# A two-layer decoder on one core: expert stages over tokens sorted by expert instead of all experts over all tokens, and gated scores computed per head

## Reference, cut to what matters

```
x = LN(x + self_attention(LN(x)))          # 16 heads of 64                      stage A
x = LN(x + cross_attention(x, ctx))        # 16 heads, 77 context rows           stage B
x = LN(x + experts(x))                     # 8 experts, width 512, gelu, the best 2 of 8      stage C
x = LN(x + gated_linear_attention(x))      # 16 heads, decay per head and row    stage D
x = LN(x + cross_attention(x, ctx))        # 8 heads                             stage E
x = LN(x + experts(x))                     # 8 experts, width 256, relu, the best 1 of 8      stage F
```

## Time and profile before

| | us |
|---|---|
| median of 3 runs | 1707.96 (1705.93 to 1708.29) |
| the profiled execution | 1707.19 |
| its span, first to last instruction | 1705.4 |
| TensorE busy | 1535.0, 90% of the span |
| VectorE, ScalarE, GpSimd busy | 964.6, 916.6, 455.8 |
| mean granted TensorE clock | 0.973 of full |

### The profile page before, as it was taken

The page is one execution under the profiler, slowest core; times in us unless marked ns, Lnnn a source line. Parts: engine busy times, 40 slices in busy tenths (PEclk is TensorE's granted clock), DMA queues, the critical chain, the costliest instruction groups (busy, mean ns, idle before and its releaser), DMA issues.

```text
span 1705.4 us, 21767 instructions
## 1 busy us (share of the span) xinstructions
PE 1535.0 (90%) x6814; PEld 833.2 (49%) x6864; DVE 964.6 (57%) x2740; ACT 916.6 (54%) x1889; POOL 455.8 (27%) x385
## 2 busy tenths in 40 slices
PE   6999999999999888878999988998889897786997
PEld 2334443444443354544555555666565663453554
DVE  3443544543443446576665647667666766466675
ACT  4777677677677354553444445556454543353433
POOL 2555455455455123230000002222222221121000
PEclk9999999999999989999999999999999997897999
DMA  4000000000000200001000000000000000100000
GB/s 145 1 1 1 1 1 1 1 1 1 1 1 1 75 25 1 0 1 62 1 0 1 1 25 1 1 1 1 1 1 1 1 1 1 50 1 0 1 13 13
DMA packets 13504, 18.56 MB, mean 11 GB/s; under 512 B 832, under 2 KB 9808, under 8 KB 13264
## 3 DMA queue, kind: packets, MB, share of 16 engines
q1 hardware_dynamic: 12816, 16.06, 3.0%
q10 hardware_dynamic: 576, 1.11, 0.2%
HBM read 16.11 MB, written 1.05 MB: 10 GB/s over the span
## 4 chain that ended last, share of the span: by engine, by line
PE 71%; DVE 16%; ACT 6%; issue 5%; POOL 0%; DMA 0%; POOLq 0%; DVEq 0%; ACTq 0%
PE bank L624 8%; PE bank L443 7%; PE bank L425 7%; PE bank L376 6%; PE bank L433 6%; PE bank L759 3%; PE bank L415 3%; PE bank L505 3%; PE bank L519 2%; PE bank L725 2%; PE bank L607 2%; PE bank L755 2%; PE bank L609 2%; PE bank L608 2%; PE bank L548 2%
## 5 line engine op out<-in xcount | busy, mean ns | idle before, releaser
L1719 POOL TENSOR_TENSOR work<-work 128x512 f32<-128x512 f32 x256 | 266.2, 1040 | 269.3 <-DVE work L1279 269.3
L892 ACT ACTIVATE work<-bank,work 128x512 f32<-128x512 f32 x256 | 176.6, 690 | 117.1 <-DVE work L1271 117.0
L1053 ACT ACTIVATE work<-bank,cols 128x512 f32<-128x512 f32 x192 | 131.8, 687 | 189.7 <-PE bank L609 189.0
L1271 DVE TENSOR_REDUCE work<-bank 128x1 f32<-128x512 f32 x256 | 176.6, 690 | 76.0 <-PE bank L425 75.7
L624 PE MATMUL bank<-work,W 128*128 128x512 f32 x384 | 199.4, 602 | 3.9 <-DVE work L1503 3.8
L1503 DVE TENSOR_TENSOR work<-work,bank 128x512 f32<-128x512 f32 x192 | 130.0, 686 | 125.1 <-ACT work L1053 123.8
L433 PEld LDWEIGHTS bank<-cst,work 128*128 128x128 f32 x1024 | 110.5, 141 | 164.5 <-issue 103.7
L1279 DVE RECIPROCAL work<-work 128x1 f32<-128x1 f32 x256 | 41.8, 163 | 223.6 <-ACT work L892 223.3
L433 PE MATMUL bank<-cst,work 128*128 128x128 f32 x1024 | 159.9, 283 | 6.7 <-ACT work L900 6.1
L900 ACT ACTIVATE work<-bank 128x512 f32<-128x512 f32 x256 | 152.7, 597 | 0.5 <-PE bank L433 0.5
L425 PE MATMUL bank<-work 64*128 64x512 f32 x512 | 144.5, 641 | 3.4 <-ACT work L892 3.4
(11 more groups left out here) (215 smaller groups left out, 2687.1 us busy)
## 6 DMA issues: line engine op xcount, KB each, us to landing
W<-in_w1T SPq DMA_DIRECT2D x1, 2048.0 KB, 8.0
x_all<-in_x SPq DMA_DIRECT2D x4, 256.0 KB, 8.7
W<-in_L_attn_Wq SPq DMA_DIRECT2D x2, 512.0 KB, 4.3
W<-in_L_attn_Wv SPq DMA_DIRECT2D x2, 512.0 KB, 6.7
W<-in_L_attn_Wo SPq DMA_DIRECT2D x2, 512.0 KB, 8.8
W<-in_L_ffn_W SPq DMA_DIRECT2D x1, 1024.0 KB, 5.8
out<-x_all SPq DMA_DIRECT2D x4, 256.0 KB, 2.3
W<-in_L_attn_Wk ACTq DMA_DIRECT2D x1, 512.0 KB, 7.7
```

What stands on the lines that cost most here:

```text
L892: A(pA[u % 5], bank[u % 3][:, :], ACT.Exp, bias=nmax[:, u % 8:u % 8 + 1], accum_out=rsum[0][:, u % 8:u % 8 + 1]).then_inc(sem("a_e"), 1)
L1053: A(hsC[i % 3], bank[i % 3][:, :], m_["func"], bias=col(m_["b1"], s)).then_inc(sem(n + "_h"), 1)
L1271: V.tensor_reduce(nmax[:, u % 8:u % 8 + 1], bank[u % 3][:, :], AX, ALU.max, negate=True)\
L1719: G.tensor_tensor(pA[u % 5], pA[u % 5], rsum[1][:, u % 8:u % 8 + 1].to_broadcast([P, S]), ALU.mult)\
```

## The change

**Experts.** The router now runs for all four sequences first, and makes for each (token, choice) pair a rank within its expert: prefix sums by TensorE (`moe_prefix`), counts by VectorE (`moe_rank`). GpSimd scatters each row of x, 128 rows per indirect DMA, to a DRAM tensor `xs`, in which each expert has its own 2048 rows (`moe_scatter`: 32 DMAs in stage C, 16 in F). `moe_map` works out from the counts which expert each of at most 39 (stage C) or 23 (stage F) tiles of 128 rows belongs to. Then, per tile: GpSimd gathers 128 rows from `xs` (three buffers); SP reads the expert's number into a register and loads that expert's whole weights with both biases (128x1156 or 128x642 elements, seven buffers); TensorE transposes the rows, makes ft hidden slices of 128x128 and the output tile, all float32, one matmul each; ScalarE applies the activation with the bias; VectorE copies the transposed rows and adds b2; SP stores the tile to `ys` in DRAM. At the end GpSimd gathers each pair's row back (`moe_gather`: 32 DMAs in C, of which 16 within stage D, and 16 in F) and VectorE adds them, weighed, to x and normalises (`close_x`). The DRAM tensor `xs` is zeroed early, by ten DMAs on SP during stage A.

**Order.** Routing of sequences 0 and 1 moves into the cross stage before, the scatter of sequence 0 too; `close_x` of sequences 1 to 3 of stage C moves into stage D, at g = 0, 4, 8. Stage D now begins behind `close_x` of sequence 0.

**Gated scores.** `qbD` and its GpSimd pass go. Each head's scores are four 128x128 matmuls over its own 64 rows, heads alternating, into a bank per head.

```diff
@@ SP @@
+            def moe_put(J):
+                sp.wait_ge(sem("M_y"), J + 1)
+                j = J % TILES0
+                sp.dma_start(T["ys"][j * P:(j + 1) * P, :], yM[J % 3]).then_inc(sem(f"M_ys{J % 3}"), 16)
...
+                for j in range(m_["tiles"]):
+                    J = m_["j0"] + j
+                    e = sp.value_load(em[0:1, j:j + 1], min_val=0, max_val=E - 1)
+                    if j >= NW:
+                        moe_put(J - NW)
+                    sp.dma_start(wM[J % NW][:, 0:m_["wide"]], T[m_["w"]][:, bass.ds(e, 1), :])\
+                        .then_inc(sem(f"M_w{J % NW}"), 16)
@@ TensorE @@
-                mm(out[:, :], high, xh_M[b % 2], start=True, stop=False)
-                mm(out[:, :], low, xh_M[b % 2], start=False, stop=False)
-                mm(out[:, :], high, xl_M[b % 2], start=False, stop=True).then_inc(sem(n + "_hp"), 1)
+                for f in range(m_["ft"]):
+                    m = mm(out[:, f * P:(f + 1) * P], wM[J % NW][:, f * P:(f + 1) * P], xTM[J % 2], start=True, stop=True)
...
+                for f in range(ft):
+                    m = mm(out[:, 0:D], hTM[J % 3][:, f * P:(f + 1) * P], wM[J % NW][:, (ft + f) * P:(ft + f + 1) * P],
+                           start=(f == 0), stop=(f == ft - 1))
...
+                for j in range(n + 3):
+                    if j < n:
+                        moe_turn(m_, j)
+                    if 1 <= j <= n:
+                        moe_h(m_, j - 1)
+                    if j >= 3:
+                        moe_y(m_, j - 3)
...
-                        m = mm(out[:, (c % 2) * 256:(c % 2 + 1) * 256], kTD[g % 2][:, c * P:(c + 1) * P],
-                               qbD[g % 2][:, c * 256:(c + 1) * 256], start=True, stop=True)
-                    m.then_inc(sem("d_s"), 1)
+                    for hh in range(2):
+                        m = mm(out[hh][:, r], kTD[g % 2][HALF[hh], r], qTD[g % 2][HALF[hh], r], start=True, stop=True)
+                m.then_inc(sem("d_s"), 1)
@@ VectorE @@
+                dve.wait_ge(sem(f"M_g{b}"), 16 * NT * 2 + 16 * NT * (m_["b0"] // NB))
+                for k in range(m_["k"]):
+                    for t in range(NT):
+                        i = V.scalar_tensor_tensor(out=res[:, t, :], in0=gathered(m_, b, t, k), scalar=w[:, t, k:k + 1],
+                                                   in1=(res if k else x)[:, t, :], op0=ALU.mult, op1=ALU.add)
...
+                ln_stats(res)
+                ln_apply(res, x).then_inc(x_ready, 1)
@@ GpSimd @@
+                        G.indirect_dma_start(T["xs"], bass.IndirectOffsetOnAxis(s1[:, pair(m_, b, t, k)], 0),
+                                             x_all[:, 4 * b + t, :], None).then_inc(sem("M_sc"), 16)
...
+                pool.wait_ge(sem("M_sc"), 16 * NB * NT * (2 + m_["b0"] // NB))
+                for j in range(m_["tiles"]):
+                    J = m_["j0"] + j
+                    if J >= 3:
+                        pool.wait_ge(sem("M_xtp"), J - 2)
+                    G.indirect_dma_start(xgM[J % 3], None, T["xs"], bass.IndirectOffsetOnAxis(xi[:, j:j + 1], 0))\
+                        .then_inc(sem(f"M_x{J % 3}"), 16)
...
+                for b in range(2 if ph == 2 else NB):
+                    moe_gather(m_, b)
...
-                    G.tensor_tensor(qbD[g % 2].rearrange("p (c h i) -> p c h i", c=NT, h=2), q, own, ALU.mult)\
-                        .then_inc(sem("d_qb"), 1)
-
+                    if g in (1, 5):
+                        moe_gather(MOE[2], 2 + g // 5)
```

More of the change, by code:

```diff
@@ L200, in decoder @@
         wqB, wkB, wvB, woB = (W1[:, i * 1024:(i + 1) * 1024] for i in range(4))
-        w1C, w2C = W0[:, 0:4096], W0[:, 4096:8192]
+        wM = [W0[:, i * WIDE:(i + 1) * WIDE] for i in range(NW)]
         woD = W1[:, 4096:5120]
@@ new lines, in moe @@
+                tail(m_["w0"] - 1, 0)
+                moe_prefix(m_, 2)
+                for s in range(1, 5):
+                    tail(m_["w0"] - 1, s)
+                moe_logits(m_, 3)
+                moe_prefix(m_, 3)
+                n = m_["tiles"]
+                for j in range(n + 3):
[5 more added lines that the diff above has]
+                        moe_y(m_, j - 3)
@@ L825, in _ @@
             moe(5)
-            for s in range(32):
-                tail(WORKS - 1, s)
         @block_ctx.scalar
@@ new lines, in moe @@
+                n, ft = m_["tiles"], m_["ft"]
+                moe_rank(m_, 1)
+                moe_route1(m_, 2)
+                moe_route2(m_, 2)
+                for s in range(3):
+                    tail(m_["w0"] - 1, s)
+                moe_rank(m_, 2)
+                for s in range(3, 5):
+                    tail(m_["w0"] - 1, s)
+                moe_route1(m_, 3)
+                moe_route2(m_, 3)
+                moe_rank(m_, 3)
+                enter(dve, ph)
+                moe_map(m_)
```

606 lines of the change are left out of this document (339 added, 267 removed).

## The result

The changed kernel takes **1638.89 us** (median of 4 runs, 1635.87 to 1640.13) against 1706.95 for the kernel before (4 runs on the same chip, 1705.93 to 1708.29): ratio 0.9598, 95% interval 0.9585 to 0.9612. The profiled execution has a span of 1638.3 us and a mean granted clock of 0.912 (0.973 before).

A forecast was written before the change was run, and what follows sets the result against it. TensorE, busy 90% of the span, was taken as the bound: 1705.4 - 61 (stage C) + 0 (D) - 21 (E, F) + 7 (clock) = 1630.4, plus 1.8 outside the span: 1632 us, range 1600 to 1660, chance 0.53.

The forecast's parts named there:

- p = 1.3: GpSimd's queue: each indirect DMA of 128 rows costs GpSimd 1.3 us, taken from its pass over 128 partitions.
- Rival 3: GpSimd's queue: indirect DMAs are dear, 3.3 us each at the upper end, kernel slower at 1787 us; chance 0.14.
- Tile of C: Expert loop of stage C: 2.5 us a tile, the middle of 2.1 and 2.9, 39 tiles 97.5 us.
- rival 1: Loop of stage C runs at the lower clock, 1.2 GHz, tiles 3.7 us apart, 1679 us; chance 0.17.
- rival 4: Stage C not shortened: SP's register reads take 2.6 us, SP 3.5 a tile, 1708 us; chance 0.05.
- Tile of F: Expert loop of stage F: SP decides with 1.9 us a tile (1.3 to 3.5), 23 tiles 43.7 us.
- End of B, +10.5: End of stage B: eight scatters ahead of the last multiplication make it end 10.5 us later, at 780.1.
- Tail and landing: Stage B's end at 780.1 to first hidden matmul at 828.2: last sequence's tail, routing, scatter with 2.3 us landing, first load.
- Stage D, 0: Stage D's length unchanged: scores win 8 us, three closings cost 8 in all, gathers cost nothing.
- rival 2: Stage D: the halves' scores overlap fully, 14 us more won, 1618 us; chance 0.11.
- E, F: Stages E and F: scatters add 7 us to E's end; kernel's end moves from 1705.4 to 1684, -21 in all.
- Clock: TensorE nearly idle for 25 us ahead of each loop of tiles lowers the granted clock: +7 us.

The follow-up runs named there:

- Experiment 3: Changed kernel with routing of sequences 0 and 1 and scatter of sequence 0 moved behind the scores of the cross attention stages: 1633.81 us, ratio 0.9589.
- experiment 1: Kernel before with only the gated scores changed (each head against its own 64 rows, GpSimd pass gone), dense experts kept: 1700.29 us, ratio 0.9963.
- experiment 6: Changed kernel with the three closings inside stage D cut in five pieces, each put ahead of the statistics of a pair: 1625.63 us, ratio 0.9535.

## Why the prediction was right, and where it was not

The time (1632 for 1638.9) and the sign came out. The mechanism held: 234 us of TensorE's work became a loop of 86, and serial stretches around it took much of the rest. That the sum came within 8 us is luck in part: errors of +10.2 (B), +12.8 (D) and +3.8 (E) stand against -10.8 (C) and the 7 us set aside for the clock. Point by point:

- **Price of an indirect DMA.** p = 1.3 was taken from a pass of GpSimd; measured 0.96 + 0.30, about 1.26, and within 0.02 of it in all three kinds (scatter, load by tile, gather back). Rival 3 (3.3) is out.
- **Tile of C.** 2.5 was predicted, from the middle between two DMA bounds; 2.1 was measured. The step that failed is the choice of the middle. That the lower bound comes out, all bytes at the best rate seen (339 GB/s), is luck in part: the loop moved 297 GB/s from 849 to 929, with the weights of seven tiles already there, and its time is 1.90 a tile of TensorE's own with short waits and a start at half clock on top. The 17 records of 0.11 were right, and with half the weights the tile is nearly that (1.94). This overpriced the loop by 16 us. The Trainium skill's page DMA: Bandwidth & Descriptors (Rules for kernel authors) has transfers below 64 KB pay mostly overhead, which no run here tests, since none in the loop is below. Of its table of measured bandwidth, 138 GB/s at 64 KB: the two of 64 KB here went through a loop that moved 280 GB/s, and the 8 us estimated from that figure did not come.
- **Rivals 1 and 4.** Clock 0.96 in the loop, with only the first tiles at half clock: rival 1 is out. The Trainium skill's page TensorE: Matmul & The Clock Gate (Loop structure matters more than you think) shows as cold a loop with a long wait for a DMA before every matmul. This loop is not of that kind, with five waits of 0.4 to 1.7 us in 39 tiles of 17 records, so it is not the case that the page describes, though the prediction took it for that, and no run here tests that rule. In C SP's issues of 0.33 follow VectorE's end of tile: rival 4 is out, though SP does read a register in each.
- **Tile of F.** 1.9, set by SP, was predicted; 1.6 was measured. The reason stands as far as the traces show: SP's own work is 1.5 us a tile and it runs behind VectorE in F. The term was too large by 7 us over the 23 tiles, as two issues take 0.33 each, not 0.43, and the register with its arithmetic 0.9, not 1.0. That the three buffers hold TensorE up at nearly the same pace was not foreseen.
- **End of B, +10.5.** It was +20.7. The scatters' share was right (8.1 us of TensorE's wait). What failed is "VectorE's ranks are ready about 756.6", which counts ten instructions behind VectorE's old work and puts the rest of the routing at nothing: it stands in VectorE's one order ahead of the sums and reciprocals that GpSimd and then TensorE wait for, and by the time of the ranks these are 7.3 us late. The ranks' own wait adds about 1.2 to that, and a lower clock in the last product 1.6. Experiment 3 confirms the place, and shows that little of it can be won: of the 14.7 us that B and the 10.9 that E end sooner, 8 and 7 come back in the serial stretches behind them.
- **Tail and landing.** From B's end to the first hidden product 48.1 us were predicted, 54.6 measured. Of the 6.5, 2.5 are the last scatter's landing (4.8 for 2.3, the store's figure of the earlier trace rows) and 2.0 the small products ahead of the output projection, which starts 3.0 us after B's end and not 1.0; the rest is the last routing and the last norm. These 6.5 and the 16 of the loop cancel in part.
- **Stage D, 0.** It was +12.8, three sizes at once. Scores: a gain of 8 was predicted, 6 came, so the size is luck, for the reason given is another. The overlap is nearly full (1.16 for sixteen records), as rival 2 says, and 20 us are saved in the scores themselves; 9 go into the wait for the gate product's bank and 5 into two steps at a lower clock (experiment 1). So rival 2 was right on the instruction and wrong on the time. Closings: 2.7 of each was predicted from VectorE's mean share. Redone from the rows (421 less 285, over 32 steps, 4.25 of idle time against 7.3) it is 3.1, still under the 4.8 (14 to 15 in all) that came; experiment 6 speaks for the place as the reason, since the idle time of VectorE stands ahead of its statistics and the closing stood behind them. Gathers: "what waits behind them is wanted a step later" was true of GpSimd's own product. Pairs 1 and 5 are nevertheless 9 us longer with them and without the closings, but spread out they gave back 1.5 us of stage D, so how much of the 9 is theirs is open.
- **E, F.** +10.8 for +7 by the same mechanism as in B (experiment 3 takes E back to 131); the end -29.0 for -28.
- **Clock.** +7 was charged for the loops. It fell rather in B (0.89 for 0.96), in D (0.94 for 0.97) and in E (0.82 for 0.89), beside the waits. Its price over the whole kernel is not isolated; for one step of stage D it is 3.0 us at 0.66 in place of 1.00 (experiment 1).

## What to carry to other kernels

An engine's mean idle share says nothing about where an added piece of work is free. Look in the trace for the wait it idles in, and put the piece ahead of that wait: three closings cost 15 us behind the statistics and 2 in pieces ahead of them. And when an engine's instruction gets shorter, look first for who it waits for next in the same step: 0.6 us a step saved on TensorE turned into 0.5 more of waiting for a bank in 14 of 31 steps. A difference of a few us in one trace can also be the granted clock: look at it for the same step in both before giving a reason.

Where work is taken away from a long stage and little is left, price the serial stretches at its ends: here two loops of 86 and 37 us stand between stretches of 154.

## What the runs showed that was not expected

- A scatter of 128 rows lands 4.8 us after the last of 32 (3.7 behind the last of 16), where a 256 KB store had 2.3.
- While eight gathers stood in a row on GpSimd's queue, VectorE and ScalarE idled 1.3 to 5.4 us, twice nearly at the same time, with no releaser in the trace; with two gathers a step it did not occur in stage D. In F's loop or behind it such waits, 1.6 to 5.3 us, stand in most of the kernels too. The cause is open.
- More buffers for a load can cost time: six made F's loop 4 us longer in both kernels in which they were tried, and the whole kernel 6 us slower in one. The reason is open; the loop's clock was lower too (0.88 and 0.86, for 0.96 and 0.94).
- A queue that only issues transfers can come close to a loop's pace: in F SP needs 1.5 of the tile's 1.6 us for a register load, its arithmetic and two issues.
